# Cross attention of a decoder: one written-out row of 32 rounds, value products in high and low parts

## What is computed

```python
def _L1_xattn_ref(hidden_states, encoder_hidden_states, Wq, Wk, Wv, Wo, gq, gk):
    ...
    q = (hidden_states @ Wq).reshape(B, Sq, H, D)
    k = (encoder_hidden_states @ Wk).reshape(B, Skv, H, D)
    v = (encoder_hidden_states @ Wv).reshape(B, Skv, H, D)
    q = rmsnorm(q, gq)
    k = rmsnorm(k, gk)
    scores = jnp.einsum('bqhd,bkhd->bhqk', q, k) * scale
    attn = jax.nn.softmax(scores, axis=-1)
    out = jnp.einsum('bhqk,bkhd->bqhd', attn, v)
    out = out.reshape(B, Sq, H * D)
    return out @ Wo
```

## Time and profile before

| what | value |
| --- | --- |
| median of three runs | 2669.71 us |
| the profiled execution | 2671.59 us, span 2669.8 us |
| mean granted TensorE clock | 0.93 |
| TensorE busy | 2235.3 us (84%) |
| VectorE busy | 1415.9 us (53%) |
| ScalarE busy | 1209.1 us (45%) |
| GpSimd busy | 911.8 us (34%) |
| the stage that is changed | from about 1232 us to 2367 us of the span |

### The profile page before, as it was taken

The page is one execution under the profiler, slowest core; times in us unless marked ns, Lnnn a source line. Parts: engine busy times, 40 slices in busy tenths (PEclk is TensorE's granted clock), DMA queues, the critical chain, the costliest instruction groups (busy, mean ns, idle before and its releaser), DMA issues. The chain is left out here.

```text
span 2669.8 us, 35727 instructions
## 1 busy us (share of the span) xinstructions
PE 2235.3 (84%) x12406; PEld 1565.7 (59%) x12440; DVE 1415.9 (53%) x2138; ACT 1209.1 (45%) x2272; POOL 911.8 (34%) x570
## 2 busy tenths in 40 slices
PE   6888888857885887885999999999999999957672
PEld 4454545436674655553677767777777677734341
DVE  3656565634555335532555565556555755543445
ACT  3636363623424635442555545554555555522312
POOL 2424242410003202201455555555555455520101
PEclk8999898978997999997999999999999999978795
DMA  2000000010001000002111211121111011130001
...
DMA packets 62365, 84.12 MB, mean 32 GB/s; under 512 B 6132, under 2 KB 41332, under 8 KB 61752
## 3 DMA queue, kind: packets, MB, share of 16 engines
...
...
## 5 line engine op out<-in xcount | busy, mean ns | idle before, releaser
L1926 DVE RECIPROCAL s_inv_sums<-banks 128x512 f32<-128x512 f32 x64 | 214.8, 3357 | 343.2 <-PE banks L2039 339.8
L1800 POOL TENSOR_TENSOR s_qk_rstd<-s_mean_sq,minus_half 128x8 f32<-128x8 f32 x64 | 118.5, 1852 | 501.9 <-DVE s_mean_sq L1913 501.9
L594 DVE TENSOR_REDUCE s_neg_max<-banks 128x1 f32<-128x512 f32 x256 | 171.6, 688 | 113.6 <-PE banks L660 112.1
L2032 PE MATMUL banks<-s_probsT,s_v 128*128 128x512 f32 x512 | 230.9, 593 | 0.0
L1863 ACT ACTIVATE s_probsT<-banks,s_minus_bound,s_qk_rstd 128x512 f32<-128x512 f32 x256 | 177.0, 782 | 92.5 <-PE banks L200 88.5
L543 ACT ACTIVATE s_probsT<-banks 128x512 f32<-128x512 f32 x256 | 147.8, 599 | 100.5 <-PE banks L674 98.6
L198 PE MATMUL banks<-s_w_proj_hi,xT_hi 128*128 (+1 forms) x512 | 170.7, 333 | 2.9 <-DVE s_ctxT_lo L1974 2.9
L1834 ACT ACTIVATE s_squares<-banks 128x512 f32<-128x512 f32 x64 | 38.2, 597 | 284.0 <-PE banks L200 284.0
L2032 PEld LDWEIGHTS banks<-s_probsT,s_v 128*128 128x128 f32 x512 | 97.5, 190 | 111.0 <-issue 108.3
L1793 POOL TENSOR_TENSOR s_w_proj_lo<-s_w_proj_raw,s_w_proj_hi 128x2048 f32 (+1 forms) x33 | 152.0, 4606 | 14.4 <-ACT s_w_proj_hi L1826 14.4
L1809 POOL TENSOR_TENSOR s_probs_pair_sums<-s_probsT 128x1024 f32<-128x1024 f32 x64 | 151.0, 2360 | 7.2 <-issue 7.2
...
## 6 DMA issues: line engine op xcount, KB each, us to landing
...
```

What stands on the lines that cost most here:

```text
L594: dve.tensor_reduce(nmax[:, h % 2, t, 0:1], ps.ap(s), AX.X, ALU.max, negate=True) \
L1800: pool.tensor_tensor(rs[:, j, :, :], ms[:, j, :, :], c.mhalf[:, 0:T * HP].rearrange("p (t h) -> p t h", h=HP), ALU.pow) \
L1926: dve.reciprocal(inv[:, h, :], pb.ap(("sum", h))).then_inc(pb.freed(("sum", h)), 1)
L2032: mm = pe.matmul(pb.ap(("o", h)), v[:, k, h * DX:(h + 1) * DX], probsT[:, h, k, :], start=(k == 0), stop=(k == T - 1))
```

## The change

The hardware loops go. A list seq is written out in Python for rounds j = 0 to 31; every engine walks the same list and does its share of each piece, in its order. The pieces are: X a turned tile of x, Cx the context's parts, WX and WO the parts of the projection and output weights, Q queries, MQ and MK mean squares and roots, NQ q times its root, KV keys and values, TQ and TK transposes, E scores and exponentials, U sums over the probability tiles, H high and low parts of the probabilities, V value product, SU sum product, R reciprocal and product, OH parts of the outputs, O output tiles, L layer norm.

- Values: v is kept as v_hi and v_lo (v_lo by VectorE from PSUM). The probabilities of a head get a high part p_h (ScalarE, four copies from SBUF) and a low part p_l (VectorE for the first head, GpSimd for the second). V is then four times split3 instead of four fp32 products. p_h and p_l hold one head, so the second head's follow V of the first.
- Sums: each head's four tiles are added in three additions 512 wide by GpSimd, with drains between.
- The outputs' high and low parts (OH) move into the next round, among its scores; output tiles O of the round before are spread over the round. The reciprocal of the second head (R, 1) stands last in a round, after all four additions of O.
- x is turned right from x_all; the copy x_cur and its DMA go, and its space holds the squares and the sums.
- Layer norm: statistics are taken after each output tile of a sequence's last round; ScalarE normalises (scale and shift), with the shift computed by VectorE in L, after R of the second head.
- PSUM: values and sums have banks 6 and 7 for themselves.

```diff
-        sq = sb("squares", [P, T, NW])
+        v_h = sb("v_hi", [P, T, NW], F32R)
+        v_l = sb("v_lo", [P, T, NW], F32R)
+        sq = c.xcur[:, 0:2, :].rearrange("p a (b n) -> p (a b) n", n=NW)
+        psum = c.xcur[:, 2:2 + HP, :]
...
-        psum2 = sb("probs_pair_sums", [P, 2, S])
-        psum1 = sb("probs_sum", [P, HP, S])
+        probs = sb("probsT", [P, HP, T, S])
+        p_h = sb("probsT_hi", [P, T, S], F32R)
+        p_l = sb("probsT_lo", [P, T, S], F32R)
         inv = sb("inv_sums", [P, HP, S])
         o_h = sb("outT_hi", [P, HP, S], F32R)
...
+        seq = [("X", 0, k) for k in range(KD)] + [("Cx", 0), ("WX", 0)]
+        for j in range(-1, N + 1):
+            now, nxt, prv = 0 <= j < N, j + 1 < N, 0 <= j - 1
+            if now:
+                seq += [("E", j, 0, k) for k in range(T)] + [("U", j, 0)]
+                for k in range(T):
+                    seq += [("E", j, 1, k), ("H", j, 0, k)]
+                    if prv and k < HP:
+                        seq.append(("OH", j - 1, k))
+                seq.append(("U", j, 1))
+            elif prv:
+                seq += [("OH", j - 1, h) for h in range(HP)]
+            if nxt:
+                seq.append(("Q", j + 1, 0))
+            if now:
+                seq += [("V", j, 0), ("SU", j, 0)] + [("H", j, 1, k) for k in range(T)] + [("R", j, 0)]
+            if prv:
+                seq.append(("O", j - 1, 0))
+            if nxt:
+                seq += [("Q", j + 1, 1), ("MQ", j + 1)]
+            if j + 2 < N:
+                if (j + 2) % G == 0:
+                    seq += [("X", (j + 2) // G, k) for k in range(KD)]
+                seq.append(("WX", j + 2))
+            if prv:
+                seq.append(("O", j - 1, 1))
+            if now:
+                seq += [("V", j, 1), ("SU", j, 1)]
+            if nxt:
+                seq += [("KV", j + 1, 0), ("KV", j + 1, 1), ("NQ", j + 1), ("KV", j + 1, 2), ("TQ", j + 1, 0),
+                        ("KV", j + 1, 3), ("MK", j + 1), ("TQ", j + 1, 1)]
+                if (j + 2) % G == 0 and j + 2 < N:
+                    seq.append(("Cx", (j + 2) // G))
+            if prv:
+                seq.append(("O", j - 1, 2))
+            if nxt:
+                seq += [("TK", j + 1, 0), ("TK", j + 1, 1)]
+            if prv:
+                seq.append(("O", j - 1, 3))
+            if now:
+                seq += [("R", j, 1), ("WO", j)]
+            if prv and j % G == 0:
+                seq.append(("L", j // G - 1))
+
+        uses, na, nb = [], 0, 0
+        for s in seq:
+            if s[0] in ("X", "Q", "KV", "TK", "TQ"):
+                uses.append((s, na % 3, 1))
+                na += 1
+            elif s[0] in ("E", "O"):
+                uses.append((s, 3 + nb % 3, 1))
+                nb += 1
+            elif s[0] in ("V", "SU"):
+                uses.append((s, 6 + int(s[0] == "SU"), 1))
+        ps.open(uses)
...
+                if ph == "WX":
+                    pool.wait_ge(*wx_hi.after(j, 1))
+                    pool.tensor_tensor(side(wx_l, j), raw_x[:, :], side(wx_h, j).bitcast(F32), ALU.subtract) \
+                        .then_inc(wx_lo.sem, 1)
+                elif ph == "WO":
+                    pool.wait_ge(*wo_hi.after(j, 1))
+                    pool.tensor_tensor(side(wo_l, j), raw_o[:, :], side(wo_h, j).bitcast(F32), ALU.subtract) \
+                        .then_inc(wo_lo.sem, 1)
+                elif ph == "MQ":
+                    rstd(0, "q", j)
+                elif ph == "MK":
+                    rstd(1, "k", j)
+                elif ph == "U":
+                    h = s[0]
+                    pool.wait_ge(*ps.released(0, ("E", j, h, T - 1)))
+                    if j > 0:
+                        pool.wait_ge(*ps.full(0, ("SU", j - 1, h)))
+                    pool.tensor_tensor(psum[:, h, :], probs[:, h, 0, :], probs[:, h, 1, :], ALU.add)
+                    pool.drain()
+                    pool.tensor_tensor(psum[:, h, :], psum[:, h, :], probs[:, h, 2, :], ALU.add)
+                    pool.drain()
+                    pool.tensor_tensor(psum[:, h, :], psum[:, h, :], probs[:, h, 3, :], ALU.add).then_inc(p_sum.sem, 1)
+                    pool.drain()
+                elif ph == "H" and s[0] == 1:
+                    k = s[1]
+                    pool.wait_ge(*p_hi.after(j, T + k + 1))
+                    pool.tensor_tensor(p_l[:, k, :], probs[:, 1, k, :], p_h[:, k, :].bitcast(F32), ALU.subtract) \
+                        .then_inc(p_lo[1].sem, 1)
+                elif ph == "L":
+                    pool.wait_ge(*var_ready.after(j, 1))
+                    pool.tensor_tensor(c.rstd[:, :], c.veps[:, :], c.mhalf[:, 0:T], ALU.pow).then_inc(rstd_ready.sem, 1)
 
         @block.scalar
...
+                elif ph == "KV":
+                    t = s[0]
+                    kv = ps.ap(("KV", j, t))
+                    act.wait_ge(*ps.full(0, ("KV", j, t)))
                     if t == 0:
-
-                        act.wait_ge(*ms_ready["q"].after(x[1], 1))
-                    s = act.activation(sq[:, t, :], pa.ap(("kv", t))[:, 0:NW], ACT.Square)
+                        act.wait_ge(*ms_ready["q"].after(j, 1))
+                    sqr = act.activation(sq[:, t, :], kv[:, 0:NW], ACT.Square)
                     if t == T - 1:
-                        s.then_inc(squared["k"].sem, 1)
-                    act.activation(kk[:, t, :], pa.ap(("kv", t))[:, 0:NW], ACT.Copy)
-                    act.activation(v[:, t, :], pa.ap(("kv", t))[:, NW:], ACT.Copy).then_inc(pa.freed(("kv", t)), 1)
-
-                def transposed_hi(nm, j):
-                    for h in range(HP):
...
+                elif ph == "E":
+                    h, k = s
+                    if h == 0 and k == 0:
+                        act.wait_ge(bound_ready, 1)
+                        act.wait_ge(*rs_ready["k"].after(j, 1))
+                    if k == 0 and j > 0:
+                        act.wait_ge(*p_sum.after(j - 1, h + 1))
+                        if h == 1:
+                            act.wait_ge(*p_lo[1].after(j - 1, T))
+                    act.wait_ge(*ps.full(0, ("E", j, h, k)))
+                    act.activation(probs[:, h, k, :], ps.ap(("E", j, h, k)), ACT.Exp, bias=bound[:, 0:1],
+                                   scale=rs[:, 1, k, h:h + 1]).then_inc(ps.freed(("E", j, h, k)), 1)
+                elif ph == "H":
+                    h, k = s
+                    if k == 0:
+                        act.wait_ge(*ps.released(0, ("E", j, h, T - 1)))
+                        if h == 1 or j > 0:
+                            act.wait_ge(*ps.full(0, ("V", j, 0) if h else ("V", j - 1, 1)))
+                    act.activation(p_h[:, k, :], probs[:, h, k, :], ACT.Copy).then_inc(p_hi.sem, 1)
+                elif ph == "OH":
+                    h = s[0]
+                    act.wait_ge(*ps.released(0, ("V", j, h)))
+                    if j > 0:
+                        act.wait_ge(*ps.full(0, ("O", j - 1, T - 1)))
                     act.activation(o_h[:, h, :], inv[:, h, :], ACT.Copy).then_inc(o_hi.sem, 1)
-
-                if y is not None:
-                    outputs_hi(0)
-                    outputs_hi(1)
-                if x is not None:
+                elif ph == "L":
+                    act.wait_ge(*nmr_ready.after(j, 1))
                     for t in range(T):
-                        keys_values(t)
-                    transposed_hi("kT", 0)
-                    transposed_hi("qT", 1)
...
+                if ph == "X":
+                    k = s[0]
+                    dve.wait_ge(*x_hi.after(j, k + 1))
+                    dve.tensor_tensor(c.xlo[:, k, :], ps.ap(("X", j, k)), c.xhi[:, k, :].bitcast(F32), ALU.subtract) \
+                       .then_inc(ps.freed(("X", j, k)), 1)
+                elif ph == "Cx":
+                    dve.wait_ge(*ctx_hi.after(j, 1))
+                    dve.tensor_tensor(c_l[:, :, :], cT[:, :, :], c_h[:, :, :].bitcast(F32), ALU.subtract).then_inc(ctx_lo.sem, 1)
+                elif ph == "MQ":
+                    mean_squares(0, "q", j)
+                elif ph == "MK":
+                    mean_squares(1, "k", j)
+                elif ph == "KV":
+                    t = s[0]
+                    dve.wait_ge(*v_hi.after(j, t + 1))
+                    dve.tensor_tensor(v_l[:, t, :], ps.ap(("KV", j, t))[:, NW:], v_h[:, t, :].bitcast(F32), ALU.subtract) \
+                       .then_inc(ps.freed(("KV", j, t)), 1)
+                elif ph == "NQ":
...
+                elif ph in ("TK", "TQ"):
+                    h = s[0]
+                    i = int(ph == "TQ")
+                    dve.wait_ge(*f_hi[ph].after(j, h + 1))
+                    if ph == "TQ":
+                        low = dve.scalar_tensor_tensor(f_l[:, i, h, :], ps.ap((ph, j, h)), gcol[:, 0:1],
+                                                       f_h[:, i, h, :].bitcast(F32), ALU.mult, ALU.subtract)
+                    else:
```

(77 more changed lines are left out.)

428 lines of the change are left out of this document (141 added, 287 removed).

## The result

The changed kernel takes 2826.16 us (median of four runs, 2824.34 to 2827.91) against 2670.60 of the kernel before in the same session (2669.33 to 2671.80): a ratio of 1.0588, 95% interval 1.0575 to 1.0602, so 155.6 us slower. The forecast was 2844, range 2695 to 2900. The profiled execution took 2827.91 us with a span of 2826.1; against the span before, +156.3. Two runs of one kernel, the first of experiment 4, took 3371.55 and 3447.56 us at a granted clock of 0.64 and 0.62, for a reason that no run shows, and are left out of all comparisons.

A forecast was written before the change was run, and what follows sets the result against it. TensorE, busy 84%, was taken as the bound. A round of 38.15 us, 4.8 more over 31 periods, gave +149; with sequence changes +21, end +7 and start -3, 2671.6 became 2845.6, stated as 2844; range 2695 to 2900.

The forecast's parts named there:

- The products alone: TensorE's own list of products in a plain round, without any waiting: 31.2 us, against a 33.35 us round before.
- First and second wait: TensorE waits for NQ ahead of TQ0, 1.45 us, and for TK0's low part ahead of the next scores, 1.04.
- The port wait: V0 waits for first-head p_l while VectorE's subtractions alternate with GpSimd's additions: 3.6 us a round, between 3.0 and 4.2.
- one addition less: VectorE gets in ahead of GpSimd's second-head sums once more, so V0 waits 3.0 us instead of 4.2.
- The clock: Granted clock falls to 1.2 GHz after TensorE's pauses at V0: 0.8 us lost a round, bounds 0 and 1.7.
- Sequence changes: Late layer norm, statistics, x transposes and clock cost 13.3 us per change, 6.9 more than before; +21 for three.
- Start -3 and end +7: Stage start without the x_cur copy: -3 us (0 to -10); stage end, with nothing filling V0's wait: +7 us.
- instruction fetch: Written-out rounds fetch more instructions; counted at nothing, since the written-out window attention stage shows no such wait.
- Order only: Rival: VectorE's subtractions and GpSimd's additions don't collide at 512 wide; round 33.75 us, total 2707, chance 0.16.
- Faster: Rival: TensorE never waits for NQ and TK0, the banks absorbing VectorE's lag; round 31.2 us, total 2628, chance 0.10.
- The second collision: Rival: NQ issues during GpSimd's 4.6 us w_proj low, holding TQ0 each round; 3.5 us more, about 2952, chance 0.08.
- the three waits: TensorE's waits each round ahead of TQ0 (1.45 us), the next scores (1.04) and V0's last blocks (3.6).

The follow-up runs named there:

- experiment 4: Changed kernel with GpSimd's additions of the probability tiles cut from 512 columns to 8: 2714.66 and 2718.87 us; with the rest filled with ones, 2716.65 us.
- experiment 8: Changed kernel with NQ early, WX held back, L late, R and OH reordered, split values kept, and sums on 8 columns of 512: 2631.77 us.
- experiment 2: Changed kernel with NQ ahead of the low parts of KV0 and KV1, and GpSimd's subtraction WX held until NQ is done: 2770.96 us.
- experiment 5: Changed kernel, still written out, with values back to fp32 products, without p_h, p_l and v_l: 2681.94 us, ratio 1.0047 to the kernel before.
- experiment 1: Changed kernel with NQ moved ahead of the low parts of KV0 and KV1 in VectorE's list, WX not held back: 2809.27 us.

## Why the prediction was right, point by point

- **The products alone, 31.2.** Reached in no plain round of any kernel here. With fp32 values the term holds (32.6 summed, 32.70 measured). Split values take 2.77 for a head instead of 3.43 (1734.75 to 1737.52 with small sums, 1744.66 to 1748.09 in the kernel with fp32 values and late L), so 0.66 of the 0.71 forecast. With the scores' 0.65 of experiment 8 taken away, its 32.21 would be 31.56; 0.36 above 31.2.
- **First and second wait.** Forecast 1.45 and 1.04 a round, measured 1.22 and 0.62 in the plain round shown, together 0.65 too much. The round without the collision is 33.78 against 33.75 all the same, and that is in part luck: 33.78 less the two waits leaves 31.94 for the products, where the forecast had 31.26 with its 0.1 for restarts. One error covers the other. That v_l ahead of NQ makes the first wait is shown (experiment 2). That the split makes the second is shown (experiment 5), not whether by v_l, by p_l or by the copies that go with them.
- **The port wait, forecast 3.6 (3.0 to 4.2).** This term was mis-sized. Periods of 36.58 with it and 33.78 without make 2.8. The mechanism was right: alternation, 1.78 for a blocked subtraction (forecast 0.55 + 1.18 = 1.73). What was wrong is how many are blocked: five of six by the forecast, four of six in the trace. The fourth subtraction (1706.45, 0.68 us) found GpSimd idle, 0.57 us ahead of its addition at 1706.55. That is the case "one addition less" for which the forecast gave 3.0, and the last low part is there at 1710.50, 13.2 us behind the round's first scores (1697.27), against 13.4 in that case. The 0.8 too much over 31 rounds is 25 us, more than the miss of 18.
- **The clock, 0.8 a round.** Measured: in 11 of 20 plain rounds 1.6, mean 0.9. The pauses ahead of it are shorter than the 2.38 of the earlier trace rows: two, of 1.33 and 0.73, with 1.7 between their ends. The round from 1317.10 has the same pauses, 1.33 ahead of 1320.25 and 0.72 ahead of 1321.94, and keeps its clock:

```profile
1322.00:1324.00 2.00, 2.00 (x7) 1.33 (x8) 0.20 (x1) 1.00 (x2) 1.31 (x2) 1.00 0.00 0
```

  Why the one round falls and the other doesn't was not found.
- **Sequence changes, 13.3 each.** The rounds of x transposes, of L and after L take 13.5 to 15.0 more than three plain rounds of 37.46. Before, they took 6.5 to 8.0 more; the difference over three changes is 21.4, against a forecast of 21. L alone was worth 21 us in the change and 33 us in the kernel with fp32 values; 24.1 us of TensorE's waits name it in both.
- **Start -3 and end +7.** The forecast counted from the first and the last scores. Counted to V0, which now has Q0 ahead of it (2.86), its start comes to about 0, and its end to 46 - 8.3 against 33.4 before, +4.3. Measured are 4.6 and 8.0 between the two profiles, so both are about 4 too low. Against the stage ahead the start cost 8.7, and some 7 of it went with the edit of experiment 2: NQ meeting WX in the first round (5.28 us of waiting instead of 1.22, so 4.1 by itself) was in the forecast as a rival for every round and not in its start. The x_cur copy, whose loss was to give 3, made TensorE wait 19.6 us before; after, three waits of 6.8, 7.3 and 8.0 stand in its place. The first of them is put down to TensorE's own sequencer; the forecast had instruction fetch at nothing, and whether this is fetch is not shown.
- **The sum.** In terms of the spans the forecast was 174 and the measurement 156.3. The plain round was 0.69 too dear, 31 times: -21.4. The first and the last period were priced as plain and are 5.2 shorter: -5.2. Sequence changes +0.4, start and end +8.6. The forecast is good to 18 us because misses of both signs met; the largest is the port wait.
- **Rivals.** "Order only" is not what happened, but its price was shown by experiment 4. "Faster" fell by its own point: TensorE waited for NQ in 31 of 31. The second collision came in the first round alone (4.45 us for NQ; 1.22 in the other 31), and in full in experiment 1. The one period of 44.2 is not it: the clock falls twice there, 3.1 us more than the 41.1 of its like. Its price in my forecast, 3.5 a round, is that of the order as it stood; where NQ comes earlier, the key and value products cover most of it.

In the forecast the three waits stood side by side, and the experiments bear that out: each of the first and the third could be taken away while the other two stayed (experiments 2 and 4). But they have one source: without the split all three all but go (experiment 5). The split saves TensorE 1.3 us a round and gives VectorE 4.4 us (four p_l of 0.69 and four v_l of 0.42), all of it ahead of something that TensorE needs.
